# Moving the softplus squares of a selective-scan kernel from PSUM to SBUF, with another hand-written order of its slots

## The reference

```python
x_in, z = jnp.split(x @ in_proj_w.T + in_proj_b, 2, axis=-1)
x_conv = silu(causal 4-tap convolution of x_in + conv_b)
x_dbl = x_conv @ x_proj_w.T               # 64 columns dt_low, 16 of B, 16 of C
dt = softplus(dt_low @ dt_proj_w.T + dt_proj_b)
A_bar = exp(dt * A);  B_bar = (A_bar - 1) / A * B
h = A_bar * h + B_bar * x_conv            # one scan over time per channel and state
y = (sum over states of h * C) + D * x_conv
out = (y * silu(z)) @ out_proj_w.T + out_proj_b
```

## Time and profile before

| | |
|---|---|
| median of 3 executions | 2841.85 us |
| profiled execution | 2841.85 us, of which the span from first to last instruction is 2840.0 us |
| TensorE matmul busy | 2558.9 us (90%) |
| VectorE busy | 2363.1 us (83%) |
| GpSimd busy | 2284.4 us (80%) |
| ScalarE busy | 1800.2 us (63%) |
| mean granted TensorE clock | 0.956 |

### The profile page before, as it was taken

One profiled execution on the slowest core, in us unless ns is written; L12 is line 12 of the kernel. 1 busy time (PEld: TensorE's weight loads), 2 busy tenths in 40 slices (PEclk: granted clock), 3 DMA queues, 4 the chain that ended last, 5 costly groups with the idle time before them and its releaser, 6 DMA issues. The chain is left out here.

```text
span 2840.0 us, 37945 instructions
## 1 busy us (share of the span) xinstructions
PE 2558.9 (90%) x9658; PEld 1453.0 (51%) x9659; DVE 2363.1 (83%) x3895; ACT 1800.2 (63%) x3530; POOL 2284.4 (80%) x2094
## 2 busy tenths in 40 slices
PE   6889999999999999999898989898989988499997
PEld 2445554545454545455454545454545444377764
DVE  3889898989898989989897989898989889366668
ACT  5676766767676768585867676767676754133348
POOL 1889898979798989898998989898989898255553
PEclk8999999999999999999999999999999988699998
DMA  3333333433344333334333343434333332766557
GB/s 85 93 106 119 100 120 102 124 100 125 95 121 110 113 113 113 115 110 115 110 108 109 110 112 113 115 115 107 119 108 119 99 111 89 208 186 185 183 185 248
DMA packets 248306, 349.34 MB, mean 123 GB/s; under 512 B 75575, under 2 KB 123323, under 8 KB 247612
## 3 DMA queue, kind: packets, MB, share of 16 engines
q1 hardware_dynamic: 231372, 301.41, 36.4%
q0 software_dynamic: 15600, 44.79, 4.5%
q10 hardware_dynamic: 1152, 1.06, 0.2%
HBM read 288.72 MB, written 58.45 MB: 122 GB/s over the span
## 5 line engine op out<-in xcount | busy, mean ns | idle before, releaser
L673 POOL TENSOR_TENSOR hc<-h,c_rep 128x512 f32<-128x512 f32 x832 | 1053.1, 1271 | 165.9 <-PE y_ps L1028 87.7
L1028 PE MATMUL y_ps<-hc,dg_inv 128*128 128x512 f32 x1664 | 870.2, 616 | 25.2 <-POOL hc L673 22.3
L656 POOL TENSOR_TENSOR h<-x_conv,b_rep 128x512 f32<-128x512 f32 x640 | 807.6, 1271 | 86.5 <-DVE h L1221 60.1
L1221 DVE TENSOR_TENSOR_SCAN h<-a_ps,carry,h 128x512 f32<-128x512 f32 x640 | 807.0, 1272 | 12.6 <-ACT score L824 10.5
L766 ACT ACTIVATE a_ps<-dt,a_mat 128x512 f32<-128x512 f32 x640 | 436.5, 685 | 482.9 <-DVE h L1221 469.0
L1050 PEld LDWEIGHTS g_ps<-b_steps,x_conv_rows 128*128 128x128 f32 x3072 | 411.2, 199 | 278.3 <-issue 278.3
L1205 DVE SCALAR_TENSOR_TENSOR h<-a_ps,h 128x512 f32<-128x512 f32 x640 | 429.7, 672 | 72.2 <-ACT a_ps L766 65.8
L1050 PE MATMUL g_ps<-b_steps,x_conv_rows 128*128 128x128 f32 x3072 | 431.2, 285 | 45.6 <-DVE h L1229 17.8
L1028 PEld LDWEIGHTS y_ps<-hc,dg_inv 128*128 128x128 f32 x1664 | 291.2, 194 | 309.8 <-issue 203.8
L766 ACT ACTIVATE h<-dt,a_mat 128x512 f32<-128x512 f32 x384 | 269.9, 711 | 2.1 <-POOL hc L673 1.4
L1103 PE MATMUL work<-x_in,dg_tap 128*128 128x512 f32 x512 | 250.0, 593 | 1.9 <-ACT x_in L894 1.1
(11 more groups left out here) (248 smaller groups left out, 3622.7 us busy)
## 6 DMA issues: line engine op xcount, KB each, us to landing
c_rep<-bc_rows SPq DMA_DIRECT2D x512, 256.0 KB, 3.4
b_rep<-bc_rows SPq DMA_DIRECT2D x320, 256.0 KB, 3.7
gathered<-slot_rows SPq DMA_DIRECT2D x144, 129.5 KB, 2.2
gathered<-y_planes SPq DMA_DIRECT2D x32, 512.0 KB, 5.6
x_t<-in_x_t SPq DMA_DIRECT2D x16, 512.0 KB, 5.0
x_tok<-in_x_tok SPq DMA_DIRECT2D x16, 512.0 KB, 4.9
out<-mixed_rows SPq DMA_DIRECT2D x16, 512.0 KB, 3.1
x_t_rows<-y_gated SPq DMA_DIRECT2D x15, 512.0 KB, 5.7
```

What stands on the lines that cost most here:

```text
L656: nc.gpsimd.tensor_tensor(h[:, i % SLOTS, e], x_conv[:, u[1] % 2, chunk(i, e)], b_rep[:, n % BS], ALU.mult).then_inc(u_ready, 1)
L673: nc.gpsimd.tensor_tensor(hc[:, i % HCS, e], h[:, i % SLOTS, e], c_rep[:, i % CS], ALU.mult).then_inc(hc_pool, 1)
L1028: nc.tensor.matmul(y_ps[:, e], by, hc[:, i % HCS, e], start=first_one, stop=(i % HALF == HALF - 1)).then_inc(summed, 1)
L1221: nc.vector.tensor_tensor_scan(slot, a_ps[:, e], slot, before_it, ALU.mult, ALU.add).then_inc(scanned, 1)
```

## The change

Four things are changed together.

1. The second square goes into the SBUF tile `poly`, and the third into `square`, in place, instead of both into `g_ps`. `softplus` reads them there: its first factor has `poly` and `x_arg` as inputs, its second `square` and `poly`. The waits that kept `g_ps` apart for this are gone: in `squared` those on `make_hc` and the carry, in `make_du` those on the softplus. One is added in `squared`: the second square waits for `dt_ready` of the chunks before, since it now overwrites `poly`.
2. All tables of slots are replaced.
3. SyncE stores the B and C rows in pair 24 and loads the parts in pair 25, before in 21 and 23.
4. Three waits of TensorE are kept for one tile only (x0, c0, t0) instead of two.

```diff
-        PLACE = [("x0", 0), ("x1", 0), ("d2", 2), ("d3", 3), ("c0", 6), ("c1", 6), ("T2", 10), ("T3", 14), ("o0", 16), ("o1",
-                 17), ("x2", 22), ("r0", 24), ("x3", 25), ("r1", 26), ("c3", 27), ("c2", 31), ("r2", 34), ("t0", 36), ("t1", 36),
-                 ("r3", 39), ("low", 39), ("lg", 40), ("d1", 46), ("bc", 46), ("d0", 47), ("z2", 50), ("pf", 52), ("z1", 52),
-                 ("z3", 54), ("z0", 54), ("T0", 61), ("T1", 61)]
...
-        A_AT = [-2, 1, -1, 4, 6, 6, 9, 11, 11, 14, 16, 17, 19, 21, 27, 26, 29, 31, 31, 35, 37, 41, 42, 44, 44, 45, 51, 53, 55,
-                56, 58, 57]
-        DU_AT = [None, None, 2, None, 6, None, None, 10, None, 13, None, None, None, 24, None, 27, None, None, 34, None, 38,
-                 None, None, 43, None, 48, None, None, None, 56, None, 58]
+        PLACE = [("x0", 0), ("d3", 2), ("d2", 3), ("x1", 4), ("c0", 5), ("c1", 8), ("T2", 13), ("T3", 14), ("o0", 14), ("o1",
+                 18), ("x2", 20), ("r0", 23), ("r1", 27), ("c2", 29), ("x3", 30), ("c3", 35), ("r2", 38), ("t1", 39), ("t0", 39),
+                 ("r3", 40), ("lg", 40), ("low", 42), ("d0", 46), ("bc", 46), ("d1", 48), ("z1", 51), ("z2", 52), ("pf", 53),
+                 ("z3", 56), ("z0", 56), ("T1", 59), ("T0", 60)]
...
+        A_AT = [-1, 1, 3, 4, 5, 7, 10, 12, 11, 13, 16, 18, 22, 20, 24, 25, 28, 31, 31, 36, 38, 39, 41, 42, 46, 45, 48, 53, 55,
+                56, 57, 58]
+        DU_AT = [None, None, 3, None, 5, None, None, 12, None, 14, None, None, None, 23, None, 29, None, None, 33, None, 37,
+                 None, None, 43, None, 47, None, None, None, 57, None, 59]
...
-        SILU_AT = (12, 36)
-        SQUARES_AT = ((51, 54, 55), (12, 18, 21))
-        LOGS_AT = ((54, 55), (22, 24))
-        TURN_AT, ENDS_AT, BOTH_AT = 45, 55, 49
+        SILU_AT = (15, 43)
+        SQUARES_AT = ((52, 53, 54), (5, 6, 13))
+        LOGS_AT = ((53, 57), (12, 16))
+        TURN_AT, ENDS_AT, BOTH_AT = 52, 61, 50
...
-                act.wait_ge(square_ready, count(n, 2 * SQUARES, g * SQUARES + 1))
-                if k == 1 and not (n[1] == 0 and g == 0):
-                    u, i = (later(n, -1), HALF + PAUSE - 1) if g == 0 else (n, PAUSE - 1)
-                    hc_wait(act, u, i)
-                    carried_wait(act, u, i)
+                act.wait_ge(square_ready, count(n, 2 * SQUARES, g * SQUARES + k))
+                out = poly if k == 1 else square
+                if k == 1:
+                    wait(act, dt_ready, count(n, CH, 2 * g))
                 root, _, _ = ATANH[k - 1]
-                nc.scalar.activation(g_ps[:], square[:], ACT.Square, scale=root, bias=shifts[:, k:k + 1]).then_inc(square_ready, 1)
+                nc.scalar.activation(out[:], square[:], ACT.Square, scale=root, bias=shifts[:, k:k + 1]).then_inc(square_ready, 1)
...
-                if i == PAUSE + 3:
-                    pe.wait_ge(softplus_step, count(u, LOGS, 2 * FACTORS))
...
+                factor, other = (poly, x_arg) if k == 0 else (square, poly)
...
-                nc.vector.scalar_tensor_tensor(out=poly[:], in0=g_ps[:], scalar=ATANH[k][2], in1=other[:],
+                nc.vector.scalar_tensor_tensor(out=poly[:], in0=factor[:], scalar=ATANH[k][2], in1=other[:],
                                                op0=ALU.add, op1=ALU.mult).then_inc(softplus_step, 1)
```

More of the change, by code:

```diff
@@ L67 @@
 BY_VECTOR = (4, 9, 15)
-PAUSE = KINDS.index("ddd")
 ND, NF = KINDS.count("d"), KINDS.count("f")
@@ L370, in mamba @@
-        TURN_AT, ENDS_AT, BOTH_AT = 45, 55, 49
-        MAX_AT, INDEX_AT, IDS_AT, CHOOSE_AT, CANDIDATES_AT, REDUCE_AT, PLACES_AT, NOTED_AT = 45, 48, 50, 52, 55, 55, 59, 62
+        PLACE = [("x0", 0), ("d3", 2), ("d2", 3), ("x1", 4), ("c0", 5), ("c1", 8), ("T2", 13), ("T3", 14), ("o0", 14), ("o1",
[3 rows of a table added]
+        U_AT = [-5, -2, None, 4, None, 6, 8, None, 12, None, 15, 18, 20, None, 26, None, 29, 32, None, 34, None, 38, 41, None,
+                45, None, 47, 50, 51, None, 55, None]
+        A_AT = [-1, 1, 3, 4, 5, 7, 10, 12, 11, 13, 16, 18, 22, 20, 24, 25, 28, 31, 31, 36, 38, 39, 41, 42, 46, 45, 48, 53, 55,
+                56, 57, 58]
@@ new lines, in mamba @@
+        DU_AT = [None, None, 3, None, 5, None, None, 12, None, 14, None, None, None, 23, None, 29, None, None, 33, None, 37,
+                 None, None, 43, None, 47, None, None, None, 57, None, 59]
+        TOKENS_AT, ROWS_OUT_AT = 9, 22
+        SCATTER_AT = (1, 2, 3, 5, 9, 10, 12, 14)
+        ADD_RELU_AT = (59, 60, 18, 20)
+        Z_AT = (49, 5)
+        STEPS_AT = (47, 48, 53, 55, 58, 63)
+        SUMS_AT = (20, 22)
+        SILU_AT = (15, 43)
+        SQUARES_AT = ((52, 53, 54), (5, 6, 13))
@@ L372, in mamba @@
+        LOGS_AT = ((53, 57), (12, 16))
+        TURN_AT, ENDS_AT, BOTH_AT = 52, 61, 50
+        MAX_AT, INDEX_AT, IDS_AT, CHOOSE_AT, CANDIDATES_AT, REDUCE_AT, PLACES_AT, NOTED_AT = 45, 47, 49, 52, 55, 60, 61, 63
         ROOT_AT, INVERSE_AT, NORMALISE_AT = 24, 26, 28
-        GATE_AT, HALO_IN_AT, HALO_OUT_AT = 59, 5, 61
-        SKIP_AT = (25, 29, 35, 39)
-        TOKENS_AT, ROWS_OUT_AT, BC_OUT_AT, PARTS_AT = 9, 23, 21, 23
+        GATE_AT, HALO_IN_AT, HALO_OUT_AT = 58, 4, 47
+        SKIP_AT = (26, 29, 39, 41)
@@ L554, in unit_program @@
                     if plan is not last:
-                        if i == BC_OUT_AT:
+                        if i == 24:
                             store_rows(u, plan)
-                        if i == PARTS_AT:
+                        if i == 25:
                             load_parts(u)
@@ L874, in squared @@
             def squared(n, g, k):
-                wait(act, softplus_step, count(n, LOGS, g * FACTORS + max(0, k - 1)))
+                wait(act, softplus_step, count(n, LOGS, g * FACTORS))
                 if k == 0:
@@ L1061, in tile @@
                     k = int(t[1])
-                    pe.wait_ge(normed, count(u, TT, 0))
+                    if k == 0:
+                        pe.wait_ge(normed, count(u, TT, 0))
                     for tt in range(TT):
@@ L1086, in tile @@
                 elif t[0] == "x":
-                    if t in ("x0", "x1") and part == 0:
+                    if t == "x0" and part == 0:
                         pe.wait_ge(x_t_in[nq], loads(n))
@@ L1096, in tile @@
                     c, k = int(t[1]), part
-                    if plan is first and c < 2 and k == 0:
+                    if plan is first and c == 0 and k == 0:
                         pe.wait_ge(diags_ready, 1)
```

8 lines of the change are left out of this document (removed).

## The result

The changed kernel takes 2891.86 us (median of 4 runs, 2887.54 to 2892.05), the kernel before 2838.44 us on the same chip: ratio 1.0191, interval 1.0178 to 1.0202. That is slower, as forecast, but by 53 us where the forecast's sum had 14: above the forecast's own range of 2850 to 2885 us, inside the wide one of 2775 to 2920. The top-8 of slot 45 comes every 150.93 us (13 units, 316.05 to 2278.09) instead of every 147.38.

A forecast was written before the change was run, and what follows sets the result against it. VectorE, GpSimd and TensorE were taken as near full in slots 0-22, TensorE and VectorE in 23-45, ScalarE as limit in 46-63. +1.3 a unit times 15, less 5.6, on 2841.85 gave 2856 us; range 2850 to 2885, wide 2775 to 2920.

The forecast's parts named there:

- `turn_ends` without a wait: In slot 52 instead of 45, `turn_ends` finds `b_end` landed; ScalarE's 4.94 us wait goes.
- ScalarE's chain: Slots 46 to 63: ScalarE's own work, 40.5 us, remains, so less than half of the join's 8 us comes back.
- The score's wait: Before slot 45's scan: the second Silu in slot 43 makes VectorE wait 3.2 instead of 0.7 us, +2.5 a unit.
- The slower squares on ScalarE: Four squares a unit into SBUF instead of PSUM: 0.3 us at most, taken as 0.
- the rival by which the port binds everywhere: VectorE's and GpSimd's losses in all four slots reach the end, 8.5 us a unit instead of 3.2: 2935 us; chance 0.20.
- The stage 46 to 63: Slots 46 to 63 last 42.9 us instead of 46.3, -3.4 a unit.
- join 29: Pair 29's `make_du` moves to slots 57 and 58, the join's own slot: +0.8 us a unit.
- the exponential of pair 27: Behind sigmoid, `choose` and a square in slots 49 to 53; named as possibly making VectorE wait much more than forecast.
- so I let them go: -1.8: Joins other than pair 25's lose their waits: earlier `make_du` and TensorE's lighter start of a unit, -1.8 us a unit.
- the port's term: SBUF squares: slots 12 and 16 cost VectorE 1.8 and GpSimd 1.4 us, slots 53 and 57 nothing; +3.2 a unit.
- The start: Before the first unit, ScalarE's and TensorE's waits for `b_end` go: -5.6 us once.
- The sum: -3.4 + 2.5 + 3.2 - 1.8 + 0.8 = +1.3 us a unit.

The follow-up runs named there:

- the hybrid: Slots 0 to 44 as in the kernel before, slots 45 to 63 as in the changed kernel: 2817.94 us, ratio 0.9918; with x_t loaded earlier 2764.01 us, 0.9749.
- yielding: The changed kernel with GpSimd's add to dt of the third chunk asked for in slot 15 instead of 18: 2883.16 us, ratio 1.0166.

## Why the prediction was right in sign and wrong in size

*Right.* The sign was right, and so was `turn_ends` without a wait. ScalarE's chain is what stays of slots 46 to 63, so that not 8 us come back. The score's wait was forecast at 3.2 us and measured at 3.17. The slower squares on ScalarE were put at nothing, and an instruction takes 1.14 us against 1.11. That the squares alone cost 3.2 us a unit in the old order, which is the forecast's term, is luck: 1.9 of them arise before slot 0, where the forecast had none. And the time lies in the range of the rival by which the port binds everywhere (above 2885 us, chance 0.20), but not by its mechanism: in slots 12 and 53 the port cost nothing.

*The stage 46 to 63* was forecast at -3.4 and +0.8 for join 29, -2.6; measured is -4.7 at slot 0. `turn_ends` alone gives -2.8. The new wait for the exponential of pair 27 (3.29 us in slot 53), which was named as a risk, is there and is part of the chain.

*The step that failed first: "so I let them go: -1.8".* TensorE's start of a unit is not lighter where it counts. It waits for x_t, and that load's time hangs on GpSimd through SyncE's queue. In the new tail it comes only 1.3 us earlier, where slot 0 comes 4.7 us earlier: +3.1 us in slots 3 and 4. The joins that the term let go (all but pair 25's) wait 60.4 us in after, and 26.2 in before: +2.3 us a unit instead of -1.8. That slots 3 and 4 are x_t's is shown by loading it earlier, in after (-3.1 at slot 4, though the whole got slower) and in the hybrid (-48 us). The wait for x_t stood in the trace of before and was in none of my sums.

*The second: the port's term, mis-sized by place.* The prediction had 0.9 us in each of slots 12 and 16, and +1.4 for GpSimd. Measured: 0 in slot 12, 4.3 in slot 16 (5.53 less 1.22), 0 in slot 53 and 0.4 in slot 57, and 1.0 us of GpSimd's. The earlier trace rows had shown a wait that ended with GpSimd's instruction, and I took this for the rule. It holds in slot 57, not in slot 16. That the length follows GpSimd's ready work is shown by yielding (1.87 us), by x_t earlier (6.84, 9.30 us), and by the last unit after, 10.21 us until GpSimd waits for this very instruction. In the usual unit VectorE gets in at the first end at which GpSimd's next product was not ready well before. Of the 5.5 us, 2 a unit reach the end (left out: -29 us); when GpSimd yields, x_tok's load in slot 20 takes the gain, when the instruction is left out, several waits do.

The Trainium skill, page "SBUF — State Buffer", section "SBUF: two separate sides", tells of an exclusive lock for the time of one instruction. The runs agree that the two engines exclude each other, but not that VectorE's turn comes at the end of GpSimd's instruction: three such ends passed in slot 16, while in slot 57 it came at the first.

*The score*, +2.5 as a term, is in the slot table (+2.5 between slots 44 and 46), but taking it away gives 0.7: TensorE's `low` is late by almost the same. *The start* gave 3.8 us of 5.6 (VectorE's first product of unit 0 starts at 64.46, before at 68.29).

*The sum* was +1.3 a unit; measured +3.55. By stages, in medians: slots 46 to 63 -4.7 (forecast -2.6), slots 0 to 44 +5.8 (forecast +1.4), slot 45 +2.5 (forecast +2.5), together +3.5. It is not settled why the new tables are 137 us worse with the old softplus slots; no run takes that apart. Nor did any run both load x_t earlier and leave out the long instructions, so the 53 us are not added up from the two. (`U_AT`, GpSimd's slots of B x, is among the tables that were replaced, though the list of moved slots does not name it.)

## What to carry to other kernels

Price a removed wait by the next thing that is late on every engine, the DMA queue too: here one load behind others in a queue was worth 48 us. Before moving an instruction, look at what the other engine that it waits for has ready just then, not at the length of one of its instructions. And change one table entry at a time: `turn_ends` alone gave -49 us, and the same edit among thirty others is in a kernel that lost 53.

## What the hardware showed that was not expected

- VectorE's instruction on 128x1024 in SBUF can be passed over at the ends of several back-to-back instructions of GpSimd: 5.53, 9.30 and 10.21 us instead of 1.22. It gets in when GpSimd waits, when GpSimd's next product has only just become ready (1.60 us in slot 57), and beside an indirect DMA's issue (1.22 us).
- A one-input `tensor_scalar` from SBUF to SBUF (668 ns at the least) is kept out too: 5.00 us in slot 16.
- Being earlier can cost more than it brings: 3.1 us of lead at slot 4 became 1.3 us more of waiting in slot 12 and up to 3.8 us more in slot 16.
